# Attention kernel: the softmax division moves from each pair of the attention to each tile of the last stage

## The reference, cut to what matters

```python
h = layernorm(x) * (1 + ca) + sa
q, k, v = h @ wq + bq, h @ wk + bk, h @ wv + bv
attn = einsum('bqhfd,bkhd->bhfqk', q, k) / sqrt(32)
att = softmax(attn, axis=-1)
a = einsum('bhfqk,bkhd->bqhfd', att, v)
x = x + ga * (a @ wo + bo)
h = layernorm(x) * (1 + cb) + sb
x = x + gb * top2_lora_experts(h)
```

## Time and profile before

| | |
|---|---|
| median of three runs | 2808.56 us (2802.67 to 2810.24) |
| the profiled execution | 2811.7 us, its span 2809.9 us |
| TensorE busy in the span | 2757.9 us (98%) |
| VectorE, ScalarE, GpSimd busy | 2181.6 (78%), 1529.6 (54%), 1908.4 us (68%) |
| mean granted TensorE clock | 0.993 |
| DMA | 307.05 MB, mean 109 GB/s |
| TensorE on the chain that ended last | 74% of the span |

### The profile page before, as it was taken

The page is one execution under the profiler, slowest core; times in us unless marked ns, Lnnn a source line. Parts: engine busy times, 40 slices in busy tenths (PEclk is TensorE's granted clock), DMA queues, the critical chain, the costliest instruction groups (busy, mean ns, idle before and its releaser), DMA issues.

```text
span 2809.9 us, 48988 instructions
## 1 busy us (share of the span) xinstructions
PE 2757.9 (98%) x14654; PEld 1701.5 (61%) x14654; DVE 2181.6 (78%) x2801; ACT 1529.6 (54%) x2963; POOL 1908.4 (68%) x710
## 2 busy tenths in 40 slices
PE   7999999999999999999999999999999999999998
PEld 4788888884444444444444444444444447888886
DVE  4433434348999999999999999999999968667665
ACT  3111111116776767777777776776767754545543
POOL 2433333317999999999999999999999985111110
PEclk9999999999999999999999999999999999999998
DMA  7544443434434344344444433444444443333231
GB/s 263 182 143 136 144 140 132 136 115 136 91 87 100 85 87 99 87 90 94 94 91 89 96 88 87 96 90 90 90 98 90 91 130 102 107 113 105 98 112 68
DMA packets 167501, 307.05 MB, mean 109 GB/s; under 512 B 49985, under 2 KB 91393, under 8 KB 159361
## 3 DMA queue, kind: packets, MB, share of 16 engines
q1 hardware_dynamic: 158352, 240.05, 29.3%
q0 software_dynamic: 9072, 66.06, 11.5%
HBM read 159.12 MB, written 79.82 MB: 85 GB/s over the span
## 4 chain that ended last, share of the span: by engine, by line
PE 74%; DVE 2%; ACT 1%; issue 1%; POOL 0%; DVEq 0%; ACTq 0%; POOLq 0%
PE back_ps L1348 21%; PE back_ps L1362 18%; PE s_ps L1322 16%; PE s_ps L1838 12%; PE back_ps L1887 2%; PE back_ps L1379 2%; PE back_ps L1859 1%; PE back_ps L1906 1%; DVE mx L1237 1%; PE back_ps L1337 0%; ACT h_t L1695 0%; PE s_ps L1411 0%; DVE a_lo L1281 0%; DVE xn L1753 0%; DVE two_sum L1252 0%
## 5 line engine op out<-in xcount | busy, mean ns | idle before, releaser
L1218 ACT ACTIVATE p_t<-back_ps 128x512 f32<-128x512 f32 x2048 | 1113.9, 596 | 432.0 <-PE back_ps L1348 390.2
L1237 DVE TENSOR_REDUCE mx<-s_ps 128x1 f32<-128x1024 f32 x1002 | 1172.3, 1208 | 84.4 <-PE s_ps L1322 76.8
L1128 POOL TENSOR_TENSOR p_sum<-p_sum,p_t 128x2048 f32<-128x2048 f32 x254 | 1166.3, 4592 | 23.0 <-ACT p_t L1218 6.5
L1348 PE MATMUL back_ps<-q_st,k_st 98*128 98x512 f32 x2048 | 812.5, 437 | 3.4 <-POOL ones L1097 2.4
L1348 PEld LDWEIGHTS back_ps<-q_st,k_st 98*128 98x128 f32 x2048 | 344.2, 188 | 593.8 <-ACT p_t L1218 496.4
L1322 PE MATMUL s_ps<-k_st,q_st 96*128 96x512 f32 x2004 | 629.3, 395 | 0.6 <-DVE mx L1237 0.4
L1362 PE MATMUL back_ps<-p_t,v_sb 128*32 128x512 f32 x4096 | 546.4, 605 | 0.0
L1322 PEld LDWEIGHTS s_ps<-k_st,q_st 96*128 96x128 f32 x2004 | 379.1, 189 | 70.6 <-DVE mx L1237 3.4
L574 POOL TENSOR_TENSOR o_lo<-side,o_hi 128x512 fp32r<-128x512 f32 x80 | 104.2, 1302 | 321.7 <-ACT o_hi L544 321.6
L1128 POOL TENSOR_TENSOR p_sum<-p_t 128x2048 f32<-128x2048 f32 x64 | 313.4, 4897 | 9.6 <-ACT p_t L1218 9.6
L1252 DVE TENSOR_REDUCE two_sum<-p_t 128x512 f32<-128x1024 f32 x256 | 317.8, 1243 | 0.9 <-ACT p_t L1218 0.9
(11 more groups left out here) (152 smaller groups left out, 2920.8 us busy)
## 6 DMA issues: line engine op xcount, KB each, us to landing
p_sum<-two_sum POOLq DMA_DIRECT2D x63, 1024.0 KB, 6.9
q_st<-q_hi_d SPq DMA_DIRECT2D x128, 256.0 KB, 4.3
stage<-w_mod SPq DMA_DIRECT2D x48, 512.0 KB, 6.2
q_hi_d<-o_hi SPq DMA_DIRECT2D x64, 256.0 KB, 2.0
q_lo_d<-o_lo SPq DMA_DIRECT2D x64, 256.0 KB, 2.0
q_st<-q_lo_d SPq DMA_DIRECT2D x64, 256.0 KB, 4.1
att_d<-a_sb SPq DMA_DIRECT2D x128, 128.0 KB, 2.3
a_f<-att_d SPq DMA_DIRECT2D x32, 512.0 KB, 4.7
```

The costliest lines, as they stand in the source:

```text
L1128: nc.gpsimd.tensor_tensor(total, before, p_t[:, kt, :, :], ALU.add).then_inc(sum_done, 1)
L1218: nc.scalar.activation(p_t[:, s, c, :], st_ps[:, c % 2, :], ACT.Exp, scale=SCALE)\
L1237: nc.vector.tensor_reduce(mx[:, slot % 2, e:e + 1], s_ps[:, e % 2, :], AX_X, ALU.max)\
L1348: nc.tensor.matmul(st_ps[:, c % 2, :], k_st[:, slot // 2, s * P:(s + 1) * P], q_st[:, slot, jj, h * QW:(h + 1) * QW], start=True, stop=True)\
```

## The change

VectorE no longer transposes the denominators. It copies den_ps to den_sb (a tensor_reduce over an axis of length 1), SP writes num (undivided) and den (one row for each head) to DRAM, and reads the den of a pair back as 128x16, spread over all partitions. VectorE takes the reciprocal in this form one pair later, and SP writes it to rden_d. In the last stage every tile loads, beside its 128 columns of num, the reciprocals of its 32 heads for its tokens, each repeated on 32 partitions: four DMAs to r_f, r_g or r_u. GpSimd multiplies a_f by it in place, ahead of ScalarE's a_hi. The first two tiles are multiplied by GpSimd in pairs 61 and 62. Cut to its core:

```diff
 # attend, SP
         def store(pair, par):
-            sp.wait_ge(a_ready, pair + 1)
+            sp.wait_ge(num_taken, pair + 1)
             for h in range(NQW):
-                sp.dma_start(att_d.rearrange("i p s -> (i p) s")[bass.ds(pair * (HEADS * HD), HEADS * HD),
+                sp.dma_start(num_d.rearrange("i p s -> (i p) s")[bass.ds(pair * (HEADS * HD), HEADS * HD),
                                                                  h * QW:(h + 1) * QW],
-                             a_sb[h * HEADS * HD:(h + 1) * HEADS * HD, par, :]).then_inc(a_out[par], 16)
+                             num_sb[h * HEADS * HD:(h + 1) * HEADS * HD, par, :]).then_inc(num_out[par], 16)
+            for h in range(NQW):
+                if h == 0:
+                    sp.wait_ge(den_taken, pair + 1)
+                elif not below(pair, 2):
+                    sp.wait_ge(rden_out, pair * 16 - 16)
+                sp.dma_start(den_d[bass.ds(pair * HEADS, HEADS), h * QW:(h + 1) * QW],
+                             den_sb[h * HEADS * HD:(h + 1) * HEADS * HD:HD, par, :]).then_inc(den_out[par], 16)
+        def load_den(pair, par):
+            sp.wait_ge(den_out[par], (pair - par) * (8 * NQW) + 16 * NQW)
+            sp.dma_start(rden[:, :], spread(den_d, pair)).then_inc(den_back, 16)
+        def store_rden(pair):
+            sp.wait_ge(rden_done, pair + 1)
+            sp.dma_start(spread(rden_d, pair), rden[:, :]).then_inc(rden_out, 16)
+        def load_r(T):
+            for j in range(REP):
+                sp.dma_start(meet.r_f[j * HD:(j + 1) * HD, :, :],
+                             rden_d[0:KT * REP, T * P:(T + 1) * P].rearrange("(k j) s -> j k s", j=REP)[j]
+                             .partition_broadcast(HD)).then_inc(meet.r_in[T % 2], 16)
...
-            if not (below(pair, 2) or is_int(pair, NPAIR - 1)):
+            if not below(pair, 4):
+                store_rden(pair - 4)
+            if not below(pair, 2):
                 store(pair - 2, slot % 2)
+            if not below(pair, 3):
+                load_den(pair - 3, 1 - slot % 2)
+            if is_int(pair, NPAIR - 2):
+                sp.wait_ge(meet.a_div_done, 1)
+                load_r(1)
...
         pairs(sp, do)
-        store(NPAIR - 2, NPAIR % 2)
-        store(NPAIR - 1, (NPAIR - 1) % 2)
+        for pair in (NPAIR - 2, NPAIR - 1):
+            store_rden(pair - 2)
+            store(pair, pair % 2)
+            load_den(pair - 1, 1 - pair % 2)
+        store_rden(NPAIR - 2)
+        sp.wait_ge(rden_out, 16 * NPAIR - 16)
+        load_den(NPAIR - 1, (NPAIR - 1) % 2)
+        store_rden(NPAIR - 1)
 # attend, GpSimd (both divide calls at the end go too)
-                if kt == DIVIDE_AFTER and not below(pair, 2):
-                    divide(pair - 2, slot % 2)
+                if kt == DIVIDE_AFTER:
+                    if is_int(pair, NPAIR - 3):
+                        divide_tile(0)
+                    if is_int(pair, NPAIR - 2):
+                        divide_tile(1)
 # attend, VectorE
+        def take_den(pair, par):
+            dve.wait_ge(sum_used, pair + 1)
...
+            nc.vector.tensor_reduce(den_sb[:, par, :], den_ps.unsqueeze(2), AX_X, ALU.max).then_inc(den_taken, 1)
+        def invert(pair):
+            dve.wait_ge(den_back, pair * 16 + 16)
+            nc.vector.reciprocal(rden[:, :], rden[:, :]).then_inc(rden_done, 1)
...
-                if s in DIVIDE_STEPS and not below(pair, 2):
-                    divide(pair - 2, DIVIDE_STEPS.index(s))
+                if s == DEN_STEP and not below(pair, 2):
+                    take_den(pair - 2, slot % 2)
+                if s == RDEN_STEP and not below(pair, 3):
+                    invert(pair - 3)
...
         add_two(NPAIR - 1, REP - 1)
+        take_den(NPAIR - 2, NPAIR % 2)
+        invert(NPAIR - 3)
+        take_den(NPAIR - 1, (NPAIR - 1) % 2)
         for pair in (NPAIR - 2, NPAIR - 1):
-            for piece in range(3):
-                divide(pair, piece)
+            invert(pair)
 # finish, SP: tile 3's reciprocals in slot 2; behind each a_f
+                if is_int(T, 7):
+                    sp.wait_ge(up_step, 3 * NB + 3)
+                load_r(T, b, t)
                 sp.wait_ge(x1_ready, T - 3)
 # finish, GpSimd
+                pool.wait_ge(a_in[u], (T - u) * 8 + 16)
+                pool.wait_ge(r_in[u], (T - u) * (8 * REP) + 16 * REP)
+                nc.gpsimd.tensor_tensor(a_f[:, u, :, :], a_f[:, u, :, :], r_at(T, t)[:, :, :], ALU.mult).then_inc(a_div_done, 1)
                 pool.wait_ge(a_hi_done, T + 1)
...
-                nc.gpsimd.memset(up_lo[ER:2 * ER, :, :].bitcast(F32), 0.0).then_inc(up_step, 1)
+                nc.gpsimd.memset(up_lo[ER:2 * ER, 0:NB - 1, :].bitcast(F32), 0.0).then_inc(up_step, 1)
 # finish, ScalarE
-                act.wait_ge(a_in[u], (T - u) * 8 + 16)
+                act.wait_ge(a_div_done, T + 1)
```

More of the change, by code:

```diff
@@ L55 @@
     a_f: Any
+    r_f: Any
+    r_g: Any
+    r_u: Any
     a_hi: Any
@@ L66 @@
     a_in: Any
+    r_in: Any
+    a_div_done: Any
     x_in: Any
@@ L833, in attend @@
 def attend(nc, ctx, x, w_o, b_o, lora_in, lora_out, mod_raw_d, mod_gate_d, ident, wo_hi, wo_lo, wo_f,
-           q_hi_d, q_lo_d, k_hi_d, k_lo_d, v_d, att_d, ahead, two_sum, back_ps, meet, p_at):
+           q_hi_d, q_lo_d, k_hi_d, k_lo_d, v_d, num_d, den_d, rden_d, ahead, two_sum, back_ps, meet, p_at):
     NIT, _, S = q_hi_d.shape
@@ L951, in attend @@
     num_taken = sem("num_taken")
[L952 to L955, removed]
+    den_taken = meet.den_taken
+    num_out = [sem(f"num_out{u}") for u in range(2)]
+    den_out = [sem(f"den_out{u}") for u in range(2)]
+    den_back = sem("den_back")
+    rden_done = sem("rden_done")
+    rden_out = meet.rden_out
     def pairs(eng, do):
@@ L1079, in do @@
                 sp.dma_start(meet.down[:, :, :], lora_in).then_inc(meet.down_in, 16)
-                store(pair - 2, slot % 2)
                 sp.wait_ge(two_done, NPAIR * REP)
@@ L1128, in do, with divide_tile @@
                 nc.gpsimd.tensor_tensor(total, before, p_t[:, kt, :, :], ALU.add).then_inc(sum_done, 1)
[L1129 to L1139 removed]
+                if kt == DIVIDE_AFTER:
[3 more added lines that the diff above has]
+                        divide_tile(1)
+        def divide_tile(T):
+            pool.wait_ge(meet.a_in[T], 16)
+            pool.wait_ge(meet.r_in[T], 16 * REP)
+            nc.gpsimd.tensor_tensor(meet.a_f[:, T, :, :], meet.a_f[:, T, :, :], meet.r_f[:, :, :], ALU.mult)\
+              .then_inc(meet.a_div_done, 1)
         pairs(pool, do)
@@ L1471, in finish @@
     NB = mod_gate_d.shape[1]
-    G = att_d.shape[0] // NB
+    G = num_d.shape[0] // NB
+    HD = 32
+    REP = P // HD
     E = 4
@@ L1581, in tile_of, with r_at @@
         return slot - lag, (b if t >= lag else b - 1), (t - lag) % TPB
+    def r_at(T, t):
+        if t % 2 == 0 or is_int(T, 1):
+            return meet.r_f
+        return meet.r_g if isinstance(T, int) and T < 7 else meet.r_u
     def batch(table, b):
@@ L1602, in do @@
             now = tile_of(slot, b, t, 0)
+            if is_int(slot, 2):
+                sp.wait_ge(meet.den_taken, num_d.shape[0] * 2)
+                load_r(3, 0, 3)
             if now and not (isinstance(now[0], int) and now[0] < 4):
@@ L1655, in do @@
                 pool.wait_ge(up_step, 3 * bb + 4)
-                up_low(bb)
+                if bb == NB - 1:
+                    pool.wait_ge(a_div_done, 6)
+                    nc.gpsimd.memset(up_lo[ER:2 * ER, bb, :].bitcast(F32), 0.0).then_inc(up_step, 1)
+                    pool.wait_ge(up_step, 3 * bb + 5)
+                    up_low(bb)
+                    pool.wait_ge(up_step, 3 * bb + 6)
+                else:
+                    up_low(bb)
+                    pool.wait_ge(up_step, 3 * bb + 5)
         def up_low(bb):
@@ L1689, in do @@
                 if is_int(T, 0):
-                    act.wait_ge(meet.a_ready, att_d.shape[0] * 2)
+                    act.wait_ge(meet.rden_out, 16 * num_d.shape[0] * 2)
                 act.wait_ge(turned, T + 1)
```

90 lines of the change are left out of this document (44 added, 46 removed).

## The result

The changed kernel takes 2911.05 us (median of 4 runs, 2906.46 to 2919.08), the kernel before, run beside it, 2808.39 us (4 runs). The ratio is 1.0372, with a 95% interval of 1.0345 to 1.04: slower by about 103 us, where the forecast was 9, its own range 4 to 16, and the dearest rival, (d), 31. The profiled execution's span is 2904.7 us, against 2809.9 before.

The account below looks back on a forecast made before the run. The prediction took TensorE, nearly always busy, to bound the kernel. Attention 0, passage +3.8, early tiles +6.1 and steady slots 0 gave +9.9, less about 1 for GpSimd's head start, +8.9: 2817.5 us, range 2812 to 2825.

Parts of the forecast that it names:

- (d): Attention: invert waits because den lands 4 us later than thought, each pair pays, 31 us, 2840; chance 0.03.
- Attention: Attention stage: TensorE's own 3.10 us step covers what VectorE and GpSimd lose or gain; cost 0, ends -2.5 and 0.
- (c): Attention: the step is paced through VectorE's maxima, so 0.78 us return per pair, 48 in all, 2770; chance 0.10.
- (b): Last stage: the steady loop binds, landing at 2618.2, 25 slots each 0.75 us longer, +19, 2837; chance 0.15.
- Steady slots: Last stage's 14.87 us slots: GpSimd's idle time hides the multiply and the loop closes without a stall; cost 0, bounds 0 and +19.
- the term for the landing: Steady slots: reciprocals add 1.4 to 3.1 us to a_f's landing at 2615.1, so 2616.5 to 2618.2; 2616.9 taken.
- Against: measured rate: Steady slots: the forecast's argument against the loop binding, from 369 GB/s that the engines moved in 2613 to 2614.
- Passage: Passage into the last stage: last inverts precede the first tile, L1733 starts 5.2 us later, xn ends +3.8; ends +1.3 and +7.
- store of rden [...] (2.3 by the att_d row): Passage: rden(62)'s store must land, taken as 2.3 us, within the chain that puts L1733 at 2322.6.
- From L1733 to xn: Passage, first tile on VectorE: the memset holds L1738, xn ends at 2333.3 against 2329.53; +1.3 if it does not hold.
- Tiles 4 to 6: Early tiles while GpSimd prepares tables: its multiplies meet VectorE's gate chain; +1.4, +3.2 and +1.5, together +6.1, ends 0 and +8.

Follow-up runs that it names:

- e3: Kernel after the change, loading 512 KB of numerators in place of the reciprocals, one DMA of 128 partitions, own addresses, values wrong: 2835.54 us, ratio 1.0105.
- e9: Kernel after, reciprocals ordered one tile earlier; tile 2's reciprocals and residuals of tiles 1 to 3 ordered behind the last store of rden: 2849.92 us, ratio 1.0154.
- e1: Kernel after the change, reciprocals not loaded from tile 4 on but once for tile 7, multiply kept, division wrong: 2837.19 us, ratio 1.011.
- e12: Kernel after, residuals of tiles 1 to 3 behind the small copies, reciprocals ordered a tile early but only after the present tile's multiply: 2840.05 us, ratio 1.0117.

## Why the prediction was wrong

**Attention: nearly right.** Cost 0 was forecast between -2.5 and 0. TensorE stayed full, but the stage took 4.8 us more, outside these ends; the cause stays open. The tensor_reduce took 0.669 us (0.62 forecast):

```profile
L1322 DVE TENSOR_REDUCE den_sb<-back_ps 128x512 f32<-128x512 f32 x61 | 40.8, 669 | 2.1 <-PE back_ps L1438 2.1
...
L1326 DVE RECIPROCAL rden<-rden 128x16 f32<-128x16 f32 x61 | 14.9, 244 | 7.4 <-DMA rden<-den_d 7.4
```

Rival (d), invert waiting in each pair, is out: invert waits in three pairs only, 7.4 us in all, and 0.2 us of them before 2180. Rival (c), 48 us back from VectorE, is out too: VectorE works 48 us less, and the stage is no shorter. (The price of (d), 2840, leaves out the 9 us of the other terms, which that of (b) includes.)

**Steady slots: this is the step that failed.** The loop was seen, and its closing point was right: the multiply has to start by 7.24 us after a_f's order, and the 7.9 us that the loop takes from there give a slot of 15.1. What was wrong is the term for the landing, "Lower bound of their time: 512 KB at 369 GB/s [...]. Upper: a_f's 4.9 less 1.8 of a small DMA = 3.1, landing 2618.2." Both ends came from transfers of another shape, and so counted bytes: they put the multiply 6.3 to 8.0 us after a_f's order, e3, which has a_f's shape, was at 6.2, and the kernel after at 9.6. The word "bound" was not earned, since no row showed four DMAs of 32 partitions reading the same 512 bytes. The argument "Against: measured rate" set aside the one thing that spoke for rival (b), that 32 partitions fetch the same bytes. So (b) named the right place and the sign, and priced it at 0.75 us a slot where it was 2.9; 69 of the 93 us are this. The order SP gives, with a_f, the reciprocals and the residual in one burst, was read for its issue time only, and the residual's slower landing was not in the sum at all.

**Passage: right place, wrong size.** VectorE's first L1833 was forecast at 2322.6 and came at 2332.88. The chain of small copies was there as described, once it ran: 3.81 and 3.07 us between inverts. Three inverts, though, stood ahead of tile 0, not "the last two". And the term "store of rden [...] (2.3 by the att_d row)" took a landing from the quiet attention; behind the bulk the store of rden that the chain begins with took 13.5 us. e9 shows it from the other side, 8.6 us with 2 MB moved behind. The wait of L2006 was forecast at 9 us and was 17.3.

**From L1733 to xn: the row nearest was the wrong one.** The forecast held L1738 (L1838 after) behind the memset. The memset ran from 2332.25 to 2334.90, and L1835, with two operands in SBUF, took 1.23 us beside it; L1838, 3.24 us, stood behind the subtraction into up_lo that ran from 2334.98:

```profile
2332.25 2.65 POOL L1733 MEMSET up_lo<- 64x3072 f32 x1
2334.98 2.57 POOL L1760 TENSOR_TENSOR up_lo<-up_f,up_hi 64x1024 fp32r<-64x1024 f32 x1
```

Here the rule that the prediction weighed (the Trainium skill, SBUF — State Buffer, "Who interferes with whom": a write-only GpSimd instruction does not hold such an instruction) was right, and the value taken against it was not. It moved little: up_lo then held L1838 for 2.0 us. From the start of the first L1833 to the end of xn 10.7 us were forecast and 10.15 measured. That this came out is luck in part, for another instruction held L1838 than the one in the sum, and xn was given 0.55 us and took 0.81. All of the term's miss, +13.5 us at the end of xn where +3.8 was forecast, is L1833's late start.

**Tiles 4 to 6.** +6.1 was forecast for them. e1, without the loads, shows 11.1 us in the three spacings behind the first order, and 11.3 us of L2017 (L1913 before) waiting for gmid in four tiles, against 3.9 in three before. The wait is the one that was forecast; which GpSimd instruction holds which tile is not shown, and this part of the remaining 31 us stays open, as does what e12 still loses at the passage (12.8 us of waiting for xn against 5.2).

## What to carry to other kernels

Price an added transfer by a row of its own shape: partitions per DMA, bytes per piece, whether addresses repeat. If no row has that shape, the upper end is open, and a loop that closes with 1 us to spare is then a forecast of slower. When a loop binds through a load, look first whether its order can move a slot ahead: that gave back 62 of 103 us without a byte less. Look also for links that are only the order of an engine's program, as std behind a_hi here. And where an engine is always busy, time the same work from end to end, since its busy share can't show that it became slower. Small copies that an engine waits for belong ahead of bulk, whichever queue issues them, and every transfer moved behind them needs its own reader looked up: here the sooner copies alone gained nothing.

## What the runs showed of the hardware

- A load of 512 KB as four DMAs of 32 partitions, all reading the same 512-byte pieces, had GpSimd's multiply start 9.6 us after a_f's order; own addresses 8.1; 4 KB pieces 7.8; one DMA of 128 partitions with own addresses 6.2.
- One DMA with 4 rows leading in its source kept 0.25 of the engines busy at 94 to 107 GB/s.
- The 8 KB store of reciprocals took 4.1 us in the median and 13.5 us behind bulk, where the 8 KB loads of den took 1.6 and the 8 KB copies into q_st 1.8.
- The first VectorE instruction behind a turn of a loop began 3.1 to 8.3 us late. One packet of kind "instruction" came 0.9 to 6.2 us into that time, and VectorE went on 2.1 to 2.7 us behind it, in all 14 kernels.
